# An adding transfer forms the result tile in place of GpSimd's sum, and the call orders of five engines are new

## What is computed

```python
x = x + _L0_conv_ref(_ln_c(x), ...)      # patches of 3 x 3 points matched with 512 prototypes
t = _to_tokens(x)
t = t + _L0_ffn_ref(_ln_t(t), W1, b1, W2, b2)   # 96 -> 384 -> 96, fp8 factors, fp16 sums
x = _from_tokens(t, x)

# _L0_conv_ref, per 3 x 3 patch of the normalised x
y = einsum('ncij,vc->nvij', patches, w_mask) / (x_norm * w_norm)
idx = argmax(y.reshape(NL, -1))          # best prototype and best point
integrate = max_act * max_sim + vc_vec * (1 - max_sim)
h = leaky_relu(concat(integrate, sim_map_max) @ w_i1.T + b_i1, 0.2)
vcs = tanh(h @ w_i2.T + b_i2)
h2 = relu(vcs @ w_l1.T + b_l1) @ w_l2.T + b_l2
out_p = einsum('ncij,oc->noij', h2.reshape(NL, 32, 3, 3), w_conv)
```

## Time and profile before

| | |
|---|---|
| median of 3 runs | 1992.98 us (1992.12 to 1996.23) |
| the profiled execution, its own time | 1996.22 us |
| its span | 1994.4 us |
| granted TensorE clock, mean | 0.985 of full speed |
| busy: PE, DVE, ACT, POOL | 95%, 94%, 83%, 81% |
| the chain that ended last: PE, DVE, issue, ACT, POOL | 72%, 10%, 6%, 5%, 3% |
| DMA, 200 to 1800 us | 49% of 16 engines, 133 GB/s |

### The profile page before, as it was taken

The page is one execution under the profiler, slowest core; times in us unless marked ns, Lnnn a source line. Parts: engine busy times, 40 slices in busy tenths (PEclk is TensorE's granted clock), DMA queues, the critical chain, the costliest instruction groups (busy, mean ns, idle before and its releaser), DMA issues.

```text
span 1994.4 us, 44820 instructions
## 1 busy us (share of the span) xinstructions
PE 1898.1 (95%) x13105; PEld 1429.9 (72%) x13105; DVE 1866.6 (94%) x6525; ACT 1656.4 (83%) x3205; POOL 1621.8 (81%) x1170
## 2 busy tenths in 40 slices
PE   5899999999999999999999999999999999999964
PEld 3567777777777777777777777777777777777642
DVE  7999999999999999999999999999999999999740
ACT  1168888888888888888888888888888888888885
POOL 2578888888888888888888888888888888888752
PEclk9999999999999999999999999999999999999985
DMA  3324545454454545445454454544545455454322
GB/s 96 100 73 129 135 125 147 117 147 125 134 139 117 150 122 139 133 127 145 116 147 126 129 143 117 146 126 133 139 119 151 118 143 129 122 150 118 92 74 71
DMA packets 83890, 249.78 MB, mean 125 GB/s; under 512 B 15736, under 2 KB 17986, under 8 KB 83650
## 3 DMA queue, kind: packets, MB, share of 16 engines
q1 hardware_dynamic: 52866, 170.80, 27.3%
q0 software_dynamic: 28672, 75.52, 18.0%
q10 hardware_dynamic: 2112, 0.60, 0.2%
HBM read 133.23 MB, written 57.02 MB: 95 GB/s over the span
## 4 chain that ended last, share of the span: by engine, by line
PE 72%; DVE 10%; issue 6%; ACT 5%; POOL 3%; DMA 2%; POOLq 0%; SPq 0%; ACTq 0%; DVEq 0%
PE y_ps L648 11%; PE y_ps L650 11%; PE y_ps L649 11%; PE bank L673 9%; PE bank L703 8%; PE bank L685 6%; PE bank L739 4%; ACT y L475 4%; PE bank L754 3%; PE bank L713 3%; DVE best_y L1025 3%; PE bank L723 2%; POOL prod L390 2%; DMA wsel<-proto_rows,w_index 1%; PE bank L711 1%
## 5 line engine op out<-in xcount | busy, mean ns | idle before, releaser
L475 ACT CAST y<-bank 128x384 f16<-128x384 f32 x1152 | 554.1, 481 | 185.9 <-PE bank L673 175.4
L1025 DVE TENSOR_REDUCE best_y<-y_ps 128x2 f32<-128x1024 f32 (+1 forms) x640 | 704.6, 1102 | 0.6 <-PE y_ps L650 0.6
L648 PE MATMUL y_ps<-proto_hi,xh 96*128 96x512 f32 x1152 | 574.1, 498 | 22.5 <-DVE best_y L1025 15.1
L483 ACT ACTIVATE h<-y,f_b 128x1152 f16<-128x1152 f16 x384 | 471.7, 1270 | 0.0
L649 PE MATMUL y_ps<-proto_lo,xh 96*128 96x512 f32 x1152 | 456.5, 396 | 0.0
L650 PE MATMUL y_ps<-proto_hi,xl 96*128 96x512 f32 x1152 | 455.9, 396 | 0.0
L673 PE MATMUL bank<-tqt,f_w 96*128 96x384 f16 x1152 | 390.2, 339 | 42.4 <-ACT y L475 34.7
L411 POOL TENSOR_TENSOR xl<-xc,xh 96x1152 fp32r<-96x1152 f32 x128 | 341.2, 2666 | 26.4 <-ACT xh L538 15.5
L343 POOL DMA_INDIRECT xsel<-x_pm,x_index x128 | 121.6, 950 | 230.0 <-DVE xn L983 216.4
L673 PEld LDWEIGHTS bank<-tqt,f_w 96*128 96x128 f16 x1152 | 110.9, 96 | 262.9 <-issue 144.4
L648 PEld LDWEIGHTS y_ps<-proto_hi,xh 96*128 96x128 f32 x1152 | 221.7, 192 | 84.1 <-issue 39.7
(11 more groups left out here) (131 smaller groups left out, 3874.7 us busy)
## 6 DMA issues: line engine op xcount, KB each, us to landing
xc<-x_cm SPq DMA_DIRECT2D x128, 432.0 KB
xp<-x_pm SPq DMA_DIRECT2D x128, 432.0 KB, 5.4
h<-h POOLq DMA_DIRECT2D x128, 432.0 KB, 4.5
out<-o_pm SPq DMA_DIRECT2D x128, 432.0 KB
xsel<-x_pm,x_index POOLq DMA_INDIRECT x128, 3.7
wsel<-proto_rows,w_index POOLq DMA_INDIRECT x128
proto_rows<-proto SPq DMA_DIRECT2D x1, 384.0 KB, 2.7
proto<-w_mask SPq DMA_DIRECT2D x1, 192.0 KB, 3.3
```

The costliest lines, as they stand in the source:

```text
L475: act.copy(y16[:, q, r * TOK:(r + 1) * TOK], bank[0][:, 0:TOK]).then_inc(s_y16, 1)
L483: act.activation(h16[:, q, :], y16[:, q, :], ACT.Relu, bias=f1_b[:, q:q + 1]).then_inc(s_h16, 1)
L648: pe.matmul(y, hi, proto_hi[:], start=True, stop=False)
L1025: dve.tensor_reduce(best_y[t % 2][:, j0:j1], y_ps[n % 2][:, 0:j1 - j0, :], AX_X, ALU.max).then_inc(s_yd, 1)
```

## The change

1. `output` on GpSimd is no sum of two tiles into `o_pm` any more, but a DMA that GpSimd issues: source `zb` (fp16, SBUF), destination `t_pm` (fp32, SBUF), adding to what stands there. Before it GpSimd waits for `zb`, for `t_pm`, and for `t_dev` (the last reader of the plain `t_pm`). `o_pm` is gone.
2. SP waits for the landing of this transfer and stores `t_pm`.
3. `ffn2_bias` waits, before it writes the single `zb`, for the landing of the previous tile's transfer; `residual(0)` waits, before it writes into a buffer of the ring, for the store of eight tiles earlier.
4. The calls in `slot` stand in another order on PE, DVE, ACT and POOL.

```diff
-        o_pm = [sb(f"o_pm{b}", [P, JC]) for b in range(2)]
-        s_o = sem("out_ready")
-        s_os = [sem(f"out_stored{b}") for b in range(2)]
+        s_o = [sem(f"t_pm_out{b}") for b in range(2)]
+        s_os = [sem(f"out_stored{b}") for b in range(RING)]
...
-                    sp.wait_ge(s_o, t + 1)
-                    sp.dma_start(out[t], o_pm[t % 2][:]).then_inc(s_os[t % 2], 16)
+                    run.landed(s_o, t)
+                    sp.dma_start(out[t], t_pm[t % RING][:]).then_inc(s_os[t % RING], 16)
...
             def output(s):
+
                 if run.live(s, STORE):
                     t = s - STORE
                     pool.wait_ge(s_zb, t + 1)
                     pool.wait_ge(s_t, 2 * (t + 1))
-                    run.landed(s_os, t - 2)
-                    pool.tensor_tensor(o_pm[t % 2][:], t_pm[t % RING][:], zb[:], ALU.add).then_inc(s_o, 1)
+                    pool.wait_ge(s_dev, t + 1)
+                    run.apart()
+                    pool.dma_start(t_pm[t % RING][:], zb[:], accum_op=ALU.add).then_inc(s_o[t % 2], 16)
...
                     dve.wait_ge(s_z, 2 * (t + 1))
-                    run.wait(s_o, t)
+                    run.landed(s_o, t - 1)
...
                     dve.wait_ge(s_cv, 2 * t + n + 1)
+                    if n == 0:
+                        run.landed(s_os, t - RING)
```

More of the change, by code:

```diff
@@ L761, in slot @@
                 ffn1(s, 0)
+                match(s, 2)
                 hidden2(s)
                 conv(s, 0)
-                match(s, 2)
+                match(s, 3)
+                turn_x(s)
                 ffn1(s, 1)
-                turn_x(s)
-                match(s, 3)
+                conv(s, 1)
+                turn_mix(s)
                 ffn1(s, 2)
-                conv(s, 1)
+                match(s, 4)
+                layer1(s)
+                match(s, 5)
                 ffn1(s, 3)
-                turn_mix(s)
-                layer1(s)
-                match(s, 4)
-                match(s, 5)
+                turn(s, 0)
+                match(s, 6)
+                turn(s, 1)
                 ffn1(s, 4)
-                turn(s, 0)
-                turn(s, 1)
+                match(s, 7)
                 ffn1(s, 5)
-                match(s, 6)
+                pick(s)
+                ffn1(s, 6)
                 hidden1(s)
-                ffn1(s, 6)
-                pick(s)
-                match(s, 7)
+                match(s, 8)
                 ffn1(s, 7)
-                match(s, 8)
                 ffn2(s, 0)
@@ L1110, in slot @@
                 x_stats(s, [3, 4])
+                x_stats(s, [5])
                 y_max(s, 2)
-                x_stats(s, [5])
+                y_max(s, 3)
+                best_v(s)
                 x_stats(s, [6, 7, 8])
+                v_index(s)
                 sims(s)
-                best_v(s)
-                y_max(s, 3)
-                v_index(s)
                 y_max(s, 4)
```

54 lines of the change are left out of this document (27 added, 27 removed).

## The result

The changed kernel takes 2040.62 us at the median of 4 runs (2036.53 to 2042.30), against 1992.55 us for the kernel before on the same chip (4 runs). The ratio is 1.0224, with a 95% interval of 1.0199 to 1.0249. The forecast was 1996 with a range up to 2024: slower than all of it. The profiled execution took 2036.5 us.

A forecast was written before the change was run, and what follows sets the result against it. PE was taken as the bound, with DVE nearly full. PE's -0.02 and DVE's +0.02 a slot gave 0; +2.7 us at the end made 1998.9, and the median, 3.2 lower, 1996 us; range 1970 to 2024.

The forecast's parts named there:

- Part 2: DVE's order: a new closed loop through y_max 3, y_max 1 and match 6, 14.5 us long; taken as +0.02 a slot.
- The 2.1: Loop's PE stretch, y_max 1's end to y_max 3: match 6, second turn, ffn1, match 7, drain; 2.1 us.
- The 12.4: Loop's DVE stretch, y_max 3 to the next slot's y_max 1: 10.1 us before, then 12.3 and 0.1 more.
- Part 5: zb on DVE moved behind t_mean, beside GpSimd's t_dev: taken as nothing; bounds nothing to 0.25 us of GpSimd's time.
- Part 1: PE's order: wait behind the turns goes, -0.21; exposed load, +0.08; two short ffn1 distances, +0.03 and +0.08.
- The sum (-0.02): PE's order alone, its gains and losses added up: -0.02 us a slot.
- first rival: PE's wait goes and nothing takes its place: a slot loses 0.11 to 0.21 us, 1974 us; chance 0.36.
- Part 3: POOL: sum's 1.83 us goes, transfer's issue adds 0.58; xl keeps 0.25 us before match 0, costing nothing.
- Part 4: Adding transfer and SP: landing 4.5 us, bounds 3.8 to 6.0; xp's slack 1.0, nothing lost; threshold 5.5.
- The one on the slow side: SP's xp load late behind a store awaiting a landing over 5.5 us: 2022 us; chance 0.26, shared with dear issue.
- xl late by 0.2: GpSimd's xl 0.2 late through the issue ahead of it; same direction and about the same price as late SP loads.
- POOL's busy time: Sign to look for in the changed kernel's profile: GpSimd's busy time down by 128 x 1.25 = 160 us.

The follow-up runs named there:

- zb_early: Changed kernel with zb's sum on DVE put back between pick_root and root 6, so GpSimd's tq starts after it; 2023.34 us, 1.0144.
- stats_only: zb_early with cos moved behind mix_sims and the last three bn_stats moved ahead of y_max 3 on DVE; 2015.29 us, 1.0093.
- after_filled: zb_early with the head of DVE's slot reordered and the last three statistics ahead of y_max 3; 1986.73 us, 0.9956.
- h_first: Changed kernel with GpSimd's issue of h's transfer put back ahead of tq; 2794.88 us, a single run.
- the pads: Two runs, kernel before plus one unread bn_stats a slot on DVE: ahead of the sum that waits for GpSimd's product, 1.0021; behind y_max 4, 1.0043.
- transfer_only: Kernel before with the adding transfer, its store and waits; call orders of before except the transfer ahead of xl; 2002.36 us, 1.0040.

## Why the prediction was wrong, step by step

- **Part 2, DVE's loop, is the term that failed most.** The loop was named rightly and sized wrongly: 12.4 + 2.1 = 14.5 against a measured 12.63 (1033.39 to 1046.02) + 2.14 = 14.77. That the two add up to the slot is so by construction, since they run from one y_max 3 to the next; that the loop holds the slot is shown by the waits at its two crossings, match 6 for y_max 1 (0.22 us) and y_max 3 for match 7 (0.13). The 2.1 holds. The 12.4 missed 0.13 for zb and some 0.1 for the small instructions, whose costs I read from the old order, where fill stood between producer and reader. I had written that 0.15 "is what one more dependent pair would add", counted one pair at 0.1, and x_dif with cos behind y_max 4 went uncounted. The part of the loop up to y_max 0 is also in a second loop, over match 4, which the prediction didn't have and zb_early ran into. Stats_only and after_filled show the size of the head: mending its order alone gave 0.26 us a slot and 1.4%.
- **Part 5, zb, was taken as nothing**: "zb starts first and GpSimd is still busy issuing h's transfer". In truth tq, which the new order puts ahead of h's transfer, still runs when zb starts, 0.3 us before tq's end. It costs 0.13 us in a plain slot and 5.3 in a bad one; zb_early is 17 us faster, and h_first shows the whole price. I had bounded what GpSimd would lose and never what DVE would.
- **Part 1, TensorE's order.** That TensorE was the bound before is borne out by the pads as far as it was tested; that it would stay the bound failed. The sum (-0.02) was small, too: the plain slot of 14.77 less the 0.22 ahead of match 6 and the 0.13 ahead of match 0 is 14.42, 0.13 under the 14.55 of before (an estimate from the medians of the starts). In the changed kernel the match between the turns has a wait of its own (TensorE's weight loads, after):

```profile
1046.08 0.19 PEld L649 LDWEIGHTS y_ps<-proto_hi,xh 96*128 96x128 f32 x1 [0.18 <-DVE best_y L1026]
```

  With DVE's order mended, the slot fell to 14.45, 0.12 under transfer_only, near the smaller end of my first rival.
- **Part 3, the issue**, was 0.58 by h's row, and is 1.00. It crossed the point that I had named ("over 0.8, match 0 is late"): from the start of ffn2's last matmul to match 0 it is 0.16 us now, where it was 0.03 (medians), and match 0 starts 0.05 us behind the end of xl, where it was 1.08. In the old orders it costs little: transfer_only is 0.4% slower, the end of the program included.
- **Part 4 was right.** Landing 3.8 us at the median, at the lower end of 3.8 to 6.0, and the statistics wait for xp 0.2 us in all, where they waited 7.4. By the Trainium skill's rule on two source reads (Collectives: The Full Stack, "The bandwidth ceiling: the fold count and why AG ≠ RS ≠ AR"), which the page states for the reduce step of a collective, it would have been 5.2 by the prediction's estimate. The trace disagrees for this transfer inside one core: 3.8, as long as the casting transfer of h takes in the same trace (3.8 at the median; before it was 4.5). By the software queue's share of the span, 29.5% now and 18.0% before, it takes 1.9 us of all 16 engines, where the prediction put 2.1.
- **The rivals.** The one on the slow side had the right sign and the wrong mechanism, by SP's loads. "xl late by 0.2" stood in it and did happen, at 0.13. The first rival, at 0.36, needed DVE to have room for TensorE's gain. DVE's 94% warned of that, and DVE's starts, which were there to be read, show only some 0.3 us of slack a slot (0.23 at the product, 0.09 at pick).
- POOL's busy time fell by 96, not 160: 128 x 0.42 = 54 of the 64 missing are the dearer issue.

Still open: which engine holds after_filled at 14.45. DVE's starts in it show no wait for another engine in the plain slot, only the 0.21 us of v_index behind top_v, which points to DVE; no run tested it. What bounded the kernel before is shown by the pads alone, and they missed their times by some 3 us.

## What to carry to other kernels

Where two engines are over 90% busy, read the start-to-start distances of the small instructions as well as the busy times and waits: time that an instruction spends waiting for its predecessor's result on the same engine is hardly in the list of waits (stats_only's has v_index behind top_v 2 times, and the starts have it in every slot). When an order is sought anew, check two things in it: that no instruction stands right behind the one whose result it reads, and that no VectorE operation with two SBUF inputs can slide beside GpSimd's work, even in the one slot where GpSimd runs late. And an exchange that looks useless or harmful alone (here the transfer) may be what lets a better order exist; it has to be tried in both.
